# A closing bias moved into the top-k tiles, and the first attention with GpSimd's half sums ahead of its product and the output bias as a TensorE product

## The chip, the cores and the metric

The kernel runs on one core of a Trainium2 chip, in one launch. The time is device microseconds. A core has five engines that run their own queues in order and meet only at semaphores: TensorE (PE; its weight loads are shown as PEld), VectorE (DVE), ScalarE (ACT), GpSimd (POOL) and SyncE (SP, which here only issues transfers).

## The reference

The input x has 2 sequences of 1024 rows of 256 numbers; the context has 2 x 77 rows of 192. Four layers are added to x one after the other, each on a layer norm of x:

```python
x = x + _L0_xattn_ref(_layernorm(x), ctx, Wq, bq, Wkv, bkv, Wo, bo)     # 16 heads of 16, softmax over 77 keys
x = x + _L0_ffn_ref(_layernorm(x), Wg, W1, b1, Wo, bo)                  # top 2 of 8 experts, gated, 512 wide
x = x + _L1_xattn_ref(_layernorm(x), ctx, masks, ...)                   # 4 heads, top 32 of 77 keys, FiLM, s4d, FFN
x = x + _L1_ffn_ref(_layernorm(x), w_gate, w_expert, b_expert)          # top 1 of 8 with capacity 100
```

The first attention ends with `attention @ Wo + bo`: this `bo` (L0_xattn_bo) is the output bias that the change moves. The third layer takes for every row and head the 32 largest of 77 scores, turns the attention into a scale and a shift (FiLM) around a long convolution (s4d, done by Fourier transforms), runs a feed-forward part of 1024 hidden units, and ends with `layernorm(xt) * g_norm_out + b_norm_out`: this `b_norm_out` is the closing bias. The experts' first bias `b1` (8 rows of 1024) is a second operand that matters here, since the change puts `bo` beside it.

## The kernel before, in words

X lies in the core's memory for the whole kernel as 16 tiles of 128 rows. The work is in stages A to F; between some of them all engines meet at a barrier (`stage_end`). Every engine's program is written out by hand, in order; nothing is scheduled by a planner. So an instruction stands where its line puts it, and a wait holds up all that is behind it on its engine.

**Stage A, the first attention.** The loop runs over 32 units u (or steps S): 4 blocks j of 4 tiles, each with 2 groups of 8 heads, so 8 units to a block. For a unit:
- TensorE makes the scores (`scores_A`).
- VectorE takes the maximum (L1642) and the difference (L1646).
- ScalarE makes the exponential (L1075).
- GpSimd halves the row for the sum: it copies the middle column (L1360) and adds the two halves (L1361) into `hsum`.
- VectorE sums what is left (`total`, L1634) and takes the reciprocal (L1636).
- GpSimd multiplies the probabilities by it (L1355, "the product").
- TensorE, three units later, transposes the probabilities (`turn_P`, L526).

In GpSimd's step S the product of unit S-1 stands first, then the copy and the half sum of unit S, then in 16 of the units `bias_A` (L1339), which adds the output bias to one tile of X. `hsum` is one buffer. After units 5 and 9 GpSimd also makes the rstd for the next blocks' layer norm (L1317 to L1322); ScalarE waits for it before it normalises (L1037). VectorE's program for unit u is: maximum and difference of u, `total(u - 1)`, layer-norm statistics in some units, `split_bias` in units 17, 21 and 25, and `add_A`, which adds the projected attention in PSUM to X (L1599) in two units of each block from the second on. `add_A` waits for `xbA`, the count of tiles that have their bias. TensorE does, beside scores and transposes, the queries of the next block, the transposes of the normalised rows z (L492 and, for the next stage, L563), `values` and `project` (products with Wo). Nearly all products share line L470, a helper.

`split_bias` cuts the experts' bias rows (`b1s`, three copies of 8 rows at partitions 0, 32 and 64) into three bf16 parts in `b1r` (L1607, L1609, and the remainder by L1531), so that stage B can add them with a bf16 product: weights `picked` (a one at the rows of the tile's expert), moving operand `b1r`. SyncE loads the biases near the start of its queue, behind X and ahead of the experts' weights, and waits for `b1r_ready` before it loads the parameters that take the place of `b1s`.

**Stage C, the top-k tiles.** For each of 16 tiles VectorE searches the 32 largest of 77 in four rounds (MAX8 L2023, MATCH_REPLACE8 L2033). GpSimd per tile: weights (L1461, waiting for ScalarE's exponentials; L1464, waiting for VectorE's L2045; L1466; L1470, for which TensorE waits to transpose at L820), then FiLM on the tile before (L1477, L1479), in two steps the sum and difference of folded tiles (L1486, 1024 elements), and the normalised rows xn (L1492). X is not written in this stage; the last reader of its tiles here is the layer norm that writes U.

**Stage D and E.** After a barrier VectorE multiplies spectra (many instructions of 128x1024 at L1531), TensorE makes Fourier products, and GpSimd adds the closing bias (`rows[:, BNO]`) to the 16 tiles of X (L1507), counted by `xbE`. The tiles are needed later, in `norm_E`.

## Time and profile before

| what | value |
|---|---|
| median of 3 runs | 807.37 us (803.51 to 812.75) |
| profiled execution, its own time | 804.53 us |
| its span | 802.7 us |
| mean granted TensorE clock | 0.92 of full |
| busy, share of the span | PE 83%, PEld 47%, DVE 69%, ACT 39%, POOL 50% |
| chain that ended last | PE 42%, DVE 32%, POOL 9%, ACT 7%, issue 5%, DMA 3% |

The span is that of the profiled execution from its first to its last instruction; the execution's own time is 1.8 us more. Busy is the time in which an engine had an instruction in work; TensorE's ends are modelled, since its products overlap. The chain is followed back from the last instruction, at each step to what released it, so it says which engine was waited for. The granted clock is TensorE's, as a share of 2.4 GHz. A unit of stage A below is named by VectorE's difference (L1646): unit 0 is at 24.4 us, unit 31 at 132.25 us.

### The profile page before, as it was taken

The page shows a single profiled execution, that of the slowest core. Times are in us where ns is not written, and L with a number is a line of the kernel's source. Part 1 is how long each engine was busy: PE and PEld are TensorE (multiplying, and loading weights), DVE is VectorE, ACT ScalarE, POOL GpSimd, SP SyncE. Part 2 cuts the span into 40 slices and gives each one's busy share as a digit, 9 for nine tenths or more (in the row PEclk, how much of TensorE's full clock was granted, in tenths as well). Part 3 has the DMA queues.
Part 4 walks back from the last instruction along what each step waited for, and adds up shares of the span by engine and source line. Part 5 has one row for each costly group of instructions (what it writes and reads, how often), then busy time and mean ns, then how long its engine had stood idle before and what let it go on. Part 6 is the DMA issues. An engine that isn't in the chain of part 4 may idle for free.

```text
span 802.7 us, 10821 instructions
## 1 busy us (share of the span) xinstructions
PE 668.8 (83%) x3380; PEld 376.3 (47%) x3380; DVE 553.8 (69%) x1694; ACT 311.6 (39%) x686; POOL 402.4 (50%) x466
## 2 busy tenths in 40 slices
PE   4879878718899898999898699875967999899971
PEld 3435435514445454545486344324423655557651
DVE  4778886393993947572587999994964994825266
ACT  2566545302828373732122577781202220031110
POOL 3789857024988787872203467975900211202120
PEclk9999999657999999999899799897996999999986
DMA  8940001111222122224790000201000000000003
GB/s 219 374 125 1 1 23 48 52 53 66 67 79 93 63 83 74 83 87 122 284 358 1 1 2 6 100 2 52 1 0 0 2 0 1 0 1 0 1 0 105
DMA packets 33087, 52.77 MB, mean 66 GB/s; under 512 B 8718, under 2 KB 21582, under 8 KB 32776
## 3 DMA queue, kind: packets, MB, share of 16 engines
q1 hardware_dynamic: 28040, 36.75, 13.8%
q0 software_dynamic: 4992, 15.34, 5.6%
q8 instruction: 28, 0.46, 0.2%
q14 instruction: 27, 0.22, 0.1%
HBM read 36.61 MB, written 15.47 MB: 65 GB/s over the span
## 4 chain that ended last, share of the span: by engine, by line
PE 42%; DVE 32%; POOL 9%; ACT 7%; issue 5%; DMA 3%; POOLq 1%; SPq 0%; DVEq 0%; ACTq 0%
PE ps L470 38%; DVE arena L1531 6%; DVE arena L2033 5%; DVE arena L2023 3%; DVE kp L1531 3%; POOL arena L1355 3%; POOL arena L1361 2%; ACT L1148 1%; DVE arena L1634 1%; DVE arena L1883 1%; ACT arena L991 1%; PE ps L776 1%; DVE X L1537 1%; ACT L1162 1%; DMA arena<-scr_g 1%
## 5 line engine op out<-in xcount | busy, mean ns | idle before, releaser
L470 PE MATMUL ps<-arena 64*32 64x32 f32 (+10 forms) x2344 | 483.7, 395 | 29.6 <-DVE arena L1820 8.7
L470 PEld LDWEIGHTS ps<-arena 64*32 64x32 f32 (+7 forms) x2344 | 227.4, 152 | 217.3 <-issue 157.7
L991 ACT ACTIVATE arena<-ps 128x512 f32<-128x512 f32 (+4 forms) x252 | 120.7, 492 | 247.4 <-PE ps L470 115.2
L331 POOL TENSOR_SCALAR rstd<-mv 128x1 f32<-128x1 f32 (+2 forms) x30 | 13.8, 458 | 225.7 <-DVE mv L325 161.8
L1883 DVE TENSOR_TENSOR arena<-ps,arena 128x512 f32<-128x512 f32 x39 | 26.9, 690 | 74.2 <-ACT arena L1148 72.4
L1404 POOL DMA_INDIRECT scr_g<-arena,destU x39 | 49.5, 1270 | 34.9 <-DVE arena L1883 25.7
L1395 POOL DMA_INDIRECT arena<-scr_z,idsU x39 | 49.1, 1260 | 22.6 <-PE ps L706 10.7
L1148 ACT ACTIVATE arena<-ps 128x512 f32<-128x512 f32 x39 | 23.3, 598 | 82.8 <-PE ps L470 82.6
L2033 DVE MATCH_REPLACE8 arena<-arena 128x77 f32<-128x77 f32 x256 | 54.1, 222 | 0.0
L1288 ACT ACTIVATE arena<-ps,b1p 128x512 f32<-128x512 f32 x32 | 22.0, 687 | 74.6 <-PE ps L470 74.6
L1355 POOL TENSOR_TENSOR arena<-arena 128x616 f32<-128x616 f32 x32 | 40.3, 1258 | 20.8 <-DVE arena L1636 19.3
L2023 DVE MAX8 arena<-arena 128x8 f32<-128x77 f32 x256 | 41.7, 224 | 1.9 <-ACT arena L1194 1.9
L1531 DVE TENSOR_TENSOR arena<-arena 128x1024 f32<-128x1024 f32 (+10 forms) x47 | 42.1, 895 | 0.8
L1531 DVE TENSOR_TENSOR arena<-arena,kp 128x1024 f32<-128x1024 f32 (+1 forms) x36 | 40.8, 1151 | 0.6
L470 PE MATMUL ps<-b1r,picked 72*128 72x512 bf16 x78 | 30.1, 386 | 8.8 <-DVE arena L1883 4.9
L1075 ACT ACTIVATE arena<-arena 128x616 f32<-128x616 f32 x32 | 22.9, 716 | 33.5 <-DVE arena L1646 33.5
L526 PE MATMUL ps<-ident,arena 128*128 128x128 f32 (+1 forms) x160 | 25.5, 292 | 10.0 <-POOL arena L1355 5.4
L470 PE MATMUL ps<-wof,arena 128*128 128x256 f32 x128 | 31.8, 395 | 0.0
L1642 DVE TENSOR_REDUCE arena<-ps 128x8 f32<-128x616 f32 x32 | 24.8, 776 | 7.5 <-PE ps L470 7.5
L333 POOL TENSOR_TENSOR rstd<-rstd,neghalf 128x1 f32<-128x1 f32 (+2 forms) x30 | 28.2, 940 | 2.5
L1507 POOL TENSOR_TENSOR X<-X,rows 128x256 f32<-128x256 f32 x16 | 25.6, 1638 | 6.6 <-POOLq L316 6.6
L336 DVE TENSOR_SCALAR arena<-X,mv,rstd 128x256 f32<-128x256 f32 x48 | 21.0, 497 | 11.1 <-POOL rstd L333 11.1
(207 smaller groups left out, 1008.9 us busy)
## 6 DMA issues: line engine op xcount, KB each, us to landing
arena<-in_w1t SPq DMA_DIRECT2D x8, 1024.0 KB, 14.0
arena<-scr_g SPq DMA_DIRECT2D x8, 1024.0 KB, 8.2
X<-in_x SPq DMA_DIRECT2D x2, 1024.0 KB, 6.3
scr_z<-arena SPq DMA_DIRECT2D x4, 512.0 KB, 2.9
arena<-in_c_dftf SPq DMA_DIRECT2D x1, 2048.0 KB, 15.6
arena<-in_L_xattn_W SPq DMA_DIRECT2D x2, 1024.0 KB, 6.3
out<-X SPq DMA_DIRECT2D x16, 128.0 KB, 1.8
scr_k<-arena SPq DMA_DIRECT2D x4, 256.0 KB, 4.6
```

Source lines behind the costliest of these rows:

```text
L333: p.tensor_tensor(rstd[:, at:at + n], rstd[:, at:at + n], neghalf[:, 0:n], ALU.pow).then_inc(s[signal], 1)
L470: return pe.matmul(o, l, r, start=first, stop=final)
L991: return a.activation(o, i, ACT.Copy)
L1148: a.activation(sig[:, u % 2, :], bank(2 * (u % 2) + 1), ACT.Sigmoid).then_inc(s["sig_ready"], 1)
L1355: p.tensor_tensor(pv, pv, smA[:, u % PBUF, :].unsqueeze(2).broadcast_to([P, HG, S2]), ALU.mult)\
L1395: p.indirect_dma_start(xg[:, st % 2, :], None, scr_z, bass.IndirectOffsetOnAxis(ap=idsU[:, st:st + 1], axis=0))\
L1404: p.indirect_dma_start(scr_g, bass.IndirectOffsetOnAxis(ap=destU[:, u:u + 1], axis=0), gt[:, u % 2, :], None).then_inc(s[f"gs{u % 2}"], 16)
L1507: p.tensor_tensor(X[:, n, :], X[:, n, :], rows[:, BNO, :], ALU.add).then_inc(s["xbE"], 1)
L1531: own.done(v.tensor_tensor(o, x, y, op))
L1883: v.tensor_tensor(gt[:, u % 2, :], bank(2 * (u % 2)), sig[:, u % 2, :], ALU.mult).then_inc(s["g_ready"], 1)
L2023: own.done(v.max(top[:, par, h, 8 * r:8 * r + 8], hv(cur)[:, h, :]))
L2033: ins = v.match_replace(hv(Rr)[:, h, :], top[:, par, h, 8 * r:8 * r + 8], hv(cur)[:, h, :], TAKEN)
```

## The change

Four things are edited together.

1. The output bias of the first attention. `bias_A` and its 16 adds go. Instead `b1r` gets one row more in front of each copy of the experts' rows (73 rows, not 72), and L0_xattn_bo is loaded there, three times, with 256 of the row's columns. `project` starts each tile's PSUM group with a bf16 product of `borow` (a one at rows 0, 32 and 64) and `b1r[:, 0:D]`. The bias row is no longer in `rows`. `project` now waits for `b1r_ready`, and `split_bias` is called in units 5, 7 and 10.
2. GpSimd's order in a step: copy and half sum of unit S first, then the product of S-1.
3. `hsum` has two buffers, the second in a part of `kp`. Before the copy GpSimd waits for `probs_sum` of unit S-2. `rstd_A` and `rstd_B` stay behind the product of units 5, 9, 16 and 24.
4. The closing bias: the 16 adds stand in the top-k tiles, each behind the xn of its tile.

```diff
@@ sync
             for i in range(3):
-                load(sp, b1s[0][32 * i:32 * i + NE, :], d["b1e"], "b1_in")
-            for i, name in enumerate(("L0_xattn_bo", "L0_ffn_bo", "L1_xattn_g_norm_in", "L1_xattn_b_norm_in",
+                load(sp, b1s[0][32 * i + 1:32 * i + 1 + NE, :], d["b1e"], "b1_in")
+                load(sp, b1s[0][32 * i:32 * i + 1, 0:D], d["L0_xattn_bo"].rearrange("(o d) -> o d", o=1), "b1_in")
+            for i, name in enumerate(("L0_ffn_bo", "L1_xattn_g_norm_in", "L1_xattn_b_norm_in",
@@ tensor, project
+                pe.wait_ge(s["b1r_ready"], 3)
                 pe.wait_ge(s["oT_sb"], 2 * j + 2)
                 for t in (2 * pair, 2 * pair + 1):
+                    o = ps[:, 6 + pair, (t % 2) * D:(t % 2) * D + D]
+                    mm(o, borow[:].broadcast_to([BROWS, P]), b1r[:, 0:D], True, False)
                     for g in range(2):
-                        ins = mm(ps[:, 6 + pair, (t % 2) * D:(t % 2) * D + D], OT[:, g, t * P:(t + 1) * P], wo0[:, g, :],
-                                 g == 0, g == 1)
+                        ins = mm(o, OT[:, g, t * P:(t + 1) * P], wo0[:, g, :], False, g == 1)
@@ gpsimd, start
+            own.done(p.memset(borow[:], 0.0))
+            own.settle()
+            for i in range(3):
+                own.done(p.memset(borow[32 * i:32 * i + 1, :], 1.0))
@@ gpsimd, stage A
             for S in range(NU + 1):
-                if S:
-                    u = S - 1
-                    p.wait_ge(s["probs_sum"], u + 1)
-                    ...
                 if S < NU:
                     p.wait_ge(s["probs_exp"], S + 1)
-                    ...
+                    if S >= 2:
+                        p.wait_ge(s["probs_sum"], S - 1)
+                    pv, hs = Pb[:, S % PBUF, :].rearrange("p (h k) -> p h k", h=HG), hsum[S % 2]
+                    p.tensor_copy(hs[:, :, H2:H2 + 1], pv[:, :, H2:H2 + 1]).then_inc(s["half_ready"], 1)
+                    p.tensor_tensor(hs[:, :, 0:H2], pv[:, :, 0:H2], pv[:, :, H2 + 1:S2], ALU.add).then_inc(s["half_ready"], 1)
                 if S == 0:
                     continue
-                if u == 0:
-                    p.wait_ge(s["rows_in"], 16 * 9)
-                if u < 5:
-                    bias_A(u)
-                ...
+                u = S - 1
+                p.wait_ge(s["probs_sum"], u + 1)
+                pv = Pb[:, u % PBUF, :].rearrange("p (h k) -> p h k", h=HG)
+                p.tensor_tensor(pv, pv, smA[:, u % PBUF, :].unsqueeze(2).broadcast_to([P, HG, S2]), ALU.mult)\
+                    .then_inc(s["probs_norm"], 1)
+                if u in (5, 9):
+                    rstd_A(2 + u // 9)
@@ gpsimd, top-k tiles
                         p.tensor_tensor(xn[:, n % 2, :], U[:, n, :], rstd[:, TB + n:TB + n + 1].broadcast_to([P, D]), ALU.mult)\
                             .then_inc(s["xn_ready"], 1)
+                        p.tensor_tensor(X[:, n, :], X[:, n, :], rows[:, BNO, :], ALU.add).then_inc(s["xbE"], 1)
@@ gpsimd, stage E
-                for n in range(NT):
-                    p.tensor_tensor(X[:, n, :], X[:, n, :], rows[:, BNO, :], ALU.add).then_inc(s["xbE"], 1)
@@ vector
-                v.wait_ge(s["xbA"], n + 2)
                 v.tensor_tensor(X[:, n:n + 2, :], X[:, n:n + 2, :], bank(6 + pair).rearrange("p (t n) -> p t n", t=2), ALU.add)\
...
-                own.done(v.tensor_reduce(smA[:, u % PBUF, :], hsum, AX, ALU.add))
+                own.done(v.tensor_reduce(smA[:, u % PBUF, :], hsum[u % 2], AX, ALU.add))
...
-                if u in (17, 21, 25):
-                    split_bias(u // 4 - 4)
+                if u in (5, 7, 10):
+                    split_bias((5, 7, 10).index(u))
```

## Rows read from the trace of the kernel before

**Rows 1.** Windows of stage A, blocks 0 to 3: length; busy PE, PEld, DVE, ACT, POOL; clock; DMA.
```profile
24.40:48.65 24.25, 20.17 (x109) 10.34 (x107) 18.23 (x39) 12.46 (x21) 19.39 (x30) 0.93 1.01 371
48.65:76.46 27.81, 24.91 (x144) 13.61 (x145) 20.79 (x44) 20.30 (x36) 24.93 (x38) 1.00 0.01 2
76.46:109.80 33.34, 25.52 (x143) 13.38 (x142) 26.96 (x47) 16.61 (x30) 24.69 (x34) 0.95 0.00 0
109.80:132.25 22.45, 20.02 (x127) 12.18 (x129) 17.93 (x37) 14.17 (x25) 16.24 (x24) 1.00 0.19 62
```

**Rows 2.** Timeline of GpSimd in a unit with the bias add: start us, us, instruction.
```profile
66.28 1.22 POOL L1355 TENSOR_TENSOR arena<-arena 128x616 f32<-128x616 f32 x1
...
68.37 0.74 POOL L1339 TENSOR_TENSOR X<-X,rows 128x256 f32<-128x256 f32 x1
69.25 1.22 POOL L1355 TENSOR_TENSOR arena<-arena 128x616 f32<-128x616 f32 x1
```

**Rows 3.** Timeline of a unit behind the last bias add; in brackets idle time, releaser.
```profile
123.56 0.72 ACT L1075 ACTIVATE arena<-arena 128x616 f32<-128x616 f32 x1 [1.46 <-DVE arena L1646]
...
124.29 0.48 DVE L1634 TENSOR_REDUCE arena<-arena 128x8 f32<-128x312 f32 x1 [0.76 <-POOL arena L1361]
...
125.08 1.22 POOL L1355 TENSOR_TENSOR arena<-arena 128x616 f32<-128x616 f32 x1 [0.83 <-DVE arena L1636]
```

**Rows 4.** Timeline of TensorE in block 1.
```profile
67.50 0.79 PE L470 MATMUL ps<-arena 64*128 64x308 f32 x4
68.22 0.77 PE L526 MATMUL ps<-ident,arena 128*128 128x128 f32 x5
68.83 1.89 PE L470 MATMUL ps<-wo,arena 128*128 128x256 f32 x8
...
72.07 2.65 PE L470 MATMUL ps<-arena 128*32 128x512 f32 x20
...
75.25 1.88 PE L470 MATMUL ps<-arena,wq 128*128 128x512 f32 x4
```

**Rows 5.** Instructions on the tile b1r: count, duration in ns min/median/max.
```profile
L1609 DVE CAST b1r<-kp x3: 637/684/1592, 81.2 to 114.5; 8x1024 bf16<-8x1024 f32 x2, 72x1024 bf16<-72x1024 f32 x1
L1531 DVE TENSOR_TENSOR kp<-kp,b1r x2: 1893/2006/2118, 81.8 to 98.7; 72x1024 f32<-72x1024 f32 x1, 8x1024 f32<-8x1024 f32 x1
L1607 DVE CAST b1r<-kp x1: 683/683/683, 96.3 to 96.3; 32x1024 bf16<-32x1024 f32 x1
```

**Rows 6.** Waits around units 7 and 21, and the window behind the second.
```profile
48.74 1.09 ACT L1037 ACTIVATE arena<-X,arena,rstd 128x256 f32<-128x256 f32 x2 [4.88 <-POOL arena L1322]
...
104.00:108.00 4.00, 3.94 (x20) 1.29 (x20) 2.82 (x7) 0.78 (x2) 3.17 (x6) 0.57 0.00 0
...
104.06 1.09 PE L563 MATMUL ps<-ident,arena 128*128 128x128 f32 x4 [4.53 <-DVE X L1599]
105.08 3.84 PE L470 MATMUL ps<-arena 128*32 128x512 f32 x20
```

**Rows 7.** Timeline of TensorE: a bf16 bias product of 512 columns, and the next.
```profile
213.19 0.38 PE L470 MATMUL ps<-b1r,picked 72*128 72x512 bf16 x1
213.41 1.88 PE L470 MATMUL ps<-arena 128*128 x4
```

**Rows 8.** Timelines of the top-k stage: a wait of GpSimd, one of TensorE.
```profile
498.73 0.84 POOL L1461 TENSOR_TENSOR arena<-arena 128x308 f32<-128x308 f32 x1 [0.80 <-ACT arena L1228]
...
509.08 0.50 PE L820 MATMUL ps<-ident,arena 128*77 128x128 f32 x1 [0.73 <-POOL arena L1470]
```

**Rows 9.** Stage D: GpSimd's adds, VectorE's products beside and behind them, TensorE.
```profile
555.33 25.65 POOL L1507 TENSOR_TENSOR X<-X,rows 128x256 f32<-128x256 f32 x16 [6.58 <-POOLq L316]
...
L1531 DVE TENSOR_TENSOR arena<-arena,kp 128x1024 f32<-128x1024 f32 x4 | 6.6, 1661 | 0.1
...
L1531 DVE TENSOR_TENSOR arena<-arena,kp 128x1024 f32<-128x1024 f32 x2 | 2.4, 1223 | 0.0
...
589.31 8.57 PE L470 MATMUL ps<-arena 128*128 128x512 f32 x16 [3.25 <-DVE arena L2124]
```

More of the change, by code:

```diff
@@ L53 @@
 SCAT = 4
-BROWS = 2 * 32 + NE
+BROWS = 2 * 32 + 1 + NE
 HUGE = 1.0e30
@@ L117, in build @@
         wx = sb("wx", [P, KD, D + NE])
-        rows = sb("rows", [P, 9, D])
-        BO0, BOF, GNI, BNI, GNO, BNO, B2, DSKIP, BEXP = range(9)
+        rows = sb("rows", [P, 8, D])
+        BOF, GNI, BNI, GNO, BNO, B2, DSKIP, BEXP = range(8)
         mgate = sb("mgate", [P, 1])
@@ L152, in build @@
         H2 = S2 // 2
-        hsum = ra.take(HG, H2 + 1)
+        hsum0 = ra.take(HG, H2 + 1)
         kvT = OT.rearrange("p g n -> p (g n)")[:, 0:4 * NB * S2].rearrange("p (a b n) -> p a b n", a=2, b=2)
@@ L207, in build @@
         erow = sb("erow", [BROWS, 1])
+        borow = sb("borow", [BROWS, 1], BF16)
         onerow = onesb[0:1, :]
@@ L219, in build @@
         kpf = kp[:].rearrange("p a b -> p (a b)")
+        hsum = (hsum0, kpf[:, 16 * P:16 * P + HG * (H2 + 1)].rearrange("p (h k) -> p h k", h=HG))
         tmpD = kpf[:, 0:2 * 4 * D].rearrange("p (i m n) -> p i m n", i=2, m=4)
@@ L423, in _ @@
                                  KT[32 * j:32 * j + 32, :, :]).then_inc(s["k_out"], 16)
-                sp.wait_ge(s["xbA"], 2 * NT)
+                sp.wait_ge(s["xbA"], NT)
                 for i in range(2):
@@ L1334, in rstd_B @@
                     ln_shift(TB + 4 * j, "lnB_stats", j + 1, "lnB_rstd")
-            def bias_A(T):
-                p.wait_ge(s["zA_ready"], T + 1)
-                p.tensor_tensor(X[:, T, :], X[:, T, :], rows[:, BO0, :], ALU.add).then_inc(s["xbA"], 1)
             rstd_A(0)
@@ L1379, in _ @@
                 rstd_B(2)
+            p.wait_ge(s["rows_in"], 16 * 8)
             stage_end("gpsimd", p)
@@ L1413, in _ @@
                         else:
-                            p.wait_ge(s["xbA"], NT + T)
+                            p.wait_ge(s["xbA"], T)
                         own.done(p.tensor_scalar(bof[:, T % 2, :], rows[:, BOF, :], cw[:, NSEL, T:T + 1], None, ALU.mult))
@@ L1602, in split_bias @@
             def split_bias(i):
-                v.wait_ge(s["b1_in"], 48)
+                v.wait_ge(s["b1_in"], 16 * 6)
                 x, rest = b1s[i % 2], b1s[(i + 1) % 2]
@@ L2357, in host_inputs @@
     o["b1e"] = A["L0_ffn_b1"]
-    o["c_erow"] = np.where(p[:BROWS] % 32 < NE, p[:BROWS] % 32, -1).astype(np.float32)[:, None]
+    o["c_erow"] = np.where(p[:BROWS] % 32 <= NE, p[:BROWS] % 32 - 1, -1).astype(np.float32)[:, None]
     o["c_iota"] = np.tile(np.arange(P, dtype=np.float32), (P, 1))
```

14 lines of the change are left out of this document (removed).

## The prediction

> **What bounds the kernel now.** The change touches three stretches: the first attention (stage A), the top-k tiles, and the head of stage D. The windows between VectorE's subtractions of units 0, 8, 16, 24 and 31 [rows 1] give blocks 0 to 2 of stage A 24.3, 27.8 and 33.3 us, and seven units of block 3 22.5. GpSimd's timeline of one unit [rows 2] shows why it looks like the limit: product 1.22 us, then column copy and half sum 1.01, bias add 0.74, and products start 2.97 us apart. Behind the last bias add the unit is as long, for another reason [rows 3]: GpSimd idles 0.83 us for VectorE's reciprocal (1.22 + 1.01 + 0.83 = 3.06), VectorE before that 0.76 us for the half sum. They wait for each other in turn. TensorE's timeline [rows 4] gives its demand: scores 0.72 us to the next start, five transposes 0.61, a projection pair 1.89, values 2.65 - 0.79 = 1.86, queries 1.88. For a block with everything in it (block 2, with 16 more transposes of z at 0.61 / 5) that is 5.8 + 4.9 + 3.8 + 3.7 + 3.8 + 2.0 = 24.0 us, 3.0 per unit. So TensorE is full at GpSimd's pace: work taken off GpSimd alone frees little in blocks 1 and 3. Block 2 is 9.3 us longer than TensorE's 24.0, and there something can be won.
>
> **Part 1, the split of the expert bias, from units 17, 21, 25 to 5, 7, 10.** Its work on VectorE [rows 5]: first part 0.64 + 2.12 = 2.8 us; second 0.68 + 1.59 + 1.89 = 4.2; third 0.68. Where it stands now TensorE idles 4.53 us for X behind the second part, comes back in a window of 4 us with a granted clock of 0.57 (mostly 1.2 GHz), and takes 3.84 us [rows 6] for the 20 instructions that took 2.65 in [rows 4]. Block 2 loses 2.8 + 4.2 + 1.2 = 8.2 us by it. Without, 25.1 us are left, just above the 24.0 that TensorE needs, so I take back all 8.2; the bounds are 4.5 (the gap alone) and 9.3.
> Block 0 has to pay. VectorE is busy 18.2 of its 24.3 us [rows 1]. Unit 5's part stands in front of the next unit's maximum, with ScalarE, GpSimd and TensorE behind it: 0 to 2.8, I take 2.8, since the neighbouring units run tight. At unit 7 ScalarE stands 4.88 us for GpSimd's rstd [rows 6], with the next exponential behind it, so the half sum comes late whatever VectorE does. The second part lies beside that wait: 0 to 4.2, I take 0.3. The third stands where TensorE is full: 0. TensorE will idle longer in block 0 than now; slow clock behind a longer gap costs between 0 and 4 x (1 - 0.57) = 1.7 us per window as in [rows 6]: 1.0. Block 0: + 4.1.
> One of the two short casts in [rows 5] takes 1.59 us where its like takes 0.68. The Trainium skill, SBUF — State Buffer, section "Who interferes with whom", has a cast of VectorE and any GpSimd instruction on one exclusive pair of ports, the later one blocked until the earlier ends; the 1.59 agrees. By that rule the first part's cast, too, can stand behind a GpSimd product of 1.22 us in its new place, and the sum below would be - 4.8 instead of - 6.0; with one cast in two seen so [rows 5], I give it half of the forecast's chance, and its 802.6 lies inside the forecast's spread.
>
> **Part 2, GpSimd's order and the second buffer.** The half sum of unit S goes ahead of the product of S-1 and needs only the exponential. In [rows 3] that ends at 124.28 us (123.56 + 0.72), while the half sum stood behind the product of 125.08. The mutual wait of 0.83 us goes, and the pace falls to that of the slowest engine: VectorE busy 17.9 us in seven units, 2.6 each; TensorE 3.0. So block 3 gains nothing. Block 1, at 27.8 against a demand of 24.0 less a z transpose, holds some stall from unit 8 on: 0 to 3.8, I take 2.0. The product comes up to 1.0 us later; TensorE transposes it three units later, which hides it, and without these units of lead it would cost 1.0 each. The wait on the sum of S-2 before the copy (for the buffer) is met already: the product of S-2, one round earlier, waited for the same count.
>
> **Part 3, the output bias.** Removed: 16 adds of 0.74 us on GpSimd, units 0 to 17, and VectorE's wait for them. TensorE being full, they are worth nothing beyond the 2.0 above. Added: 16 bf16 products of 256 columns. A bf16 product of 512 columns is followed by the next after 0.22 us [rows 7]: lower bound 0.11; upper bound a float32 step of 256 columns, 1.89 / 8 = 0.24 [rows 4]. I take 0.13, by the bf16 row as the same kind: + 2.1, all of it on TensorE's path (12 products in blocks 1 to 3, 4 in the tail). The projection's wait for b1r is met by unit 10; the first projection stands at unit 13. SyncE issues three 1 KB loads more and one of 128 KB less, in the first 13 us; the split needs them at about 40 us, and what is queued behind comes about 1 us later and is needed in later stages: 0. The four small memsets stand in GpSimd's wait for the first statistics: 0; were that cover gone, some 0.1 us each. SyncE's wait for b1r is met 50 us sooner; its parameter loads find no user before the next stage: 0.
>
> **Part 4, the closing bias.** In the top-k stage VectorE sets the pace; GpSimd idles 0.80 us before L1461 in a settled tile [rows 8], so an add of 0.74 hides. Not around 503 to 513 us, where two adds of 1024 elements fill GpSimd and TensorE idles 0.73 us for its L1470 [rows 8]: + 0.7, and + 0.5 at the last tile, which has no next tile to catch up in. Bounds: 0, and at the 25.65 / 16 = 1.60 us that each takes now [rows 9], 16 x (1.60 - 0.80) = 12.8. I take + 1.2, since GpSimd's other adds there run beside the same VectorE searches at their plain length.
> In stage D the adds cover 25.65 us, and VectorE's products of 1024 elements take 1.66 us beside them, 1.22 behind them [rows 9]; 14 of about that size make some 6 us. TensorE waits only 3.25 us for VectorE, at 589.31 [rows 9], and then sets that step itself: - 3.2 (bounds 0 and - 3.25).
>
> **Sum.** Stage A - 8.2 + 4.1 - 2.0 + 2.1 = - 4.0; top-k + 1.2; D - 3.2: - 6.0 us. The profiled execution took 804.53 us: 798.5. The median of the three runs, 807.37, is 2.8 above it: 801.4, so 801.
>
> **Rivals.** (a) Full gain: TensorE's steps in [rows 4] are stretched, and VectorE's 2.6 us per unit is the pace. Units 8 to 31 less the 2.0 counted: 23 x 0.4 = 9 us, 7 more, and the bias products hide: total about - 14, 793. For: ends of TensorE's rows are modelled. Against: its steps stand back to back, with no idle time at their side. 0.22.
> (b) Slower: the second part is not covered, and TensorE falls to 1.2 GHz before block 1, where it is the limit. Block 0 pays 7.0, two slow windows 3.4, block 1 gains nothing and block 2 only the gap of 4.5: 7.0 + 3.4 - 4.5 + 2.1 = + 8.0, with - 2.0 elsewhere + 6, 813. It decides from where block 0 and 1 lose more than the 8.2 of block 2. For: the slow return of [rows 6]. Against: ScalarE's wait is there anyway. The Trainium skill, TensorE: Matmul & The Clock Gate, section "What's actually happening", has the throttled clock as the default that activity lifts; the 0.57 behind the gap agrees. 0.10.
> (c) The new order does nothing, and the mutual wait stays in another guise: block 1's 2.0 and about 2 of block 2 are lost, 805. Against: the exponential of [rows 3] ends 0.8 us ahead of the product that it had to follow. 0.13.
> (d) The forecast: 0.55.
>
> **Numbers.** A measurement of this kernel tells about 1% (8 us) from no change. Below 799.3: (a) and a third of (d), 0.40. Above 815.4: half of (b) and the bound of part 4, 0.06. Between: 0.54. Leaving out half of (a) and most of (b): 792 to 810.
>
> **What would show it.** Right: block 2 at about 25.5 us, block 0 at 28 to 29, TensorE's gap of 4.5 us gone and one of about 5 us near unit 7; TensorE without idle in blocks 1 and 3; in D VectorE's products at 1.22 throughout and TensorE's wait of 3.25 gone; the top-k stage about 1 us longer. Wrong: units well below 3 us (a), a low granted clock in block 1 (b), or half sums that start no sooner after the exponential (c).

## The result, and the profile after

The kernel after takes **800.21 us**, the median of 11 runs (798.55 to 804.27); the kernel before took 808.37 beside it. The ratio is 0.9915, with a 95% interval of 0.9889 to 0.9941. Run a second time, unchanged, beside the experiments (a2_after), it gave 0.9939 [0.9912, 0.9965]. So it is some 0.6 to 0.9% faster, 5 to 7 us. The prediction said 801.0, with a range of 792 to 810. The profiled execution took 798.55 us against 804.53 before, 6.0 less, and the sum of the prediction's terms was -6.0. Most of what follows is about why that agreement is partly luck.

From the page of after, the busy times and the chain:

```profile
PE 667.7 (84%) x3396; PEld 376.2 (47%) x3396; DVE 545.6 (68%) x1694; ACT 312.1 (39%) x686; POOL 377.0 (47%) x454
...
PE 48%; DVE 27%; ACT 8%; POOL 7%; issue 5%; DMA 3%; POOLq 1%; SPq 0%; DVEq 0%; ACTq 0%
```

GpSimd has lost the sixteen adds of stage A and the stretched adds of stage D. Of these only 0.7 us, in stage A, had been on the chain of the kernel before. Where the 6 us came from is seen by laying the two traces' landmarks side by side. Each row gives the length of a stretch; stage A is counted between VectorE's subtractions of unit 0 and unit 31, as in [rows 1].

| stretch | before | after | difference |
|---|---|---|---|
| start to unit 0 | 24.41 | 23.61 | -0.80 |
| units 0 to 31 | 107.84 | 102.60 | -5.24 |
| unit 31 to the first gather by ids | 46.62 | 47.51 | +0.89 |
| to the first tile of top-k | 267.22 | 267.85 | +0.63 |
| top-k, to TensorE's first column of stage D | 109.16 | 110.97 | +1.81 |
| stage D, to TensorE's first product of E | 58.24 | 55.13 | -3.11 |
| the rest | 189.21 | 188.93 | -0.28 |

The windows of stage A in after answer to [rows 1]; the columns are the same (length, busy PE, PEld, DVE, ACT, POOL, clock, DMA):

```profile
23.61:49.68 26.07, 20.14 (x108) 10.02 (x106) 23.19 (x44) 12.34 (x21) 19.41 (x24) 0.87 0.99 355
49.68:79.78 30.10, 26.05 (x146) 14.44 (x147) 21.81 (x46) 19.89 (x36) 21.08 (x33) 0.94 0.04 12
79.78:104.85 25.07, 24.43 (x149) 13.58 (x148) 20.21 (x42) 17.34 (x31) 19.22 (x29) 1.00 0.06 22
104.85:126.21 21.36, 19.76 (x127) 12.30 (x125) 17.41 (x36) 13.57 (x25) 16.26 (x26) 1.00 0.08 26
```

Block 2 gained 8.3 us. The prediction had 7.7: 8.2 for the split, less 0.5 for four bias products. Blocks 0 and 1 together lost 4.1 where 2.6 was predicted. Block 0 is 1.8 longer, not 4.1; its first unit alone came out 1.1 us shorter (2.63 against 3.69), and there traces of one program differ by as much. Block 1, forecast 1.5 shorter, is 2.3 longer. Block 3, forecast 0.5 longer by its bias products, is 1.1 shorter.

GpSimd's new order is visible at once. This is the timeline of after in block 3, answering to [rows 3]: start us, us, instruction, and in brackets the idle time with what ended it.

```profile
117.29 0.71 ACT L1080 ACTIVATE arena<-arena 128x616 f32<-128x616 f32 x1
...
118.06 0.20 POOL L1360 COPY arena<-arena 128x8 f32<-128x8 f32 x1
118.21 0.83 POOL L1361 TENSOR_TENSOR arena<-arena 128x304 f32<-128x304 f32 x1
119.01 1.21 POOL L1367 TENSOR_TENSOR arena<-arena 128x616 f32<-128x616 f32 x1
...
119.27 0.47 DVE L1628 TENSOR_REDUCE arena<-arena 128x8 f32<-128x312 f32 x1
```

The exponential ends at 118.00, the half sum starts right behind it, and the product follows without the wait of 0.83 us for the reciprocal. The mutual wait is gone, so rival (c) is out for this place.

**Where blocks 0 and 1 lose.** The same timeline of after, units 5 to 9:

```profile
39.10 0.64 DVE L1603 CAST b1r<-kp 73x1024 bf16<-73x1024 f32 x1
39.77 1.89 DVE L1526 TENSOR_TENSOR kp<-kp,b1r 73x1024 f32<-73x1024 f32 x1
...
40.53 2.20 POOL L1367 TENSOR_TENSOR arena<-arena 128x616 f32<-128x616 f32 x1
...
42.79 1.33 PE L529 MATMUL ps<-ident,arena 128*128 128x128 f32 x5 [2.90 <-POOL arena L1367]
44.05 4.54 PE L473 MATMUL ps<-arena 128*32 128x512 f32 x20
...
46.10 0.74 DVE L1601 CAST b1r<-kp 32x1024 bf16<-32x1024 f32 x1
46.26 0.67 POOL L1326 TENSOR_SCALAR rstd<-mv 128x4 f32<-128x4 f32 x1
47.01 0.64 POOL L1327 TENSOR_SCALAR arena<-mv 128x4 f32<-128x4 f32 x1
47.59 1.22 DVE L1526 TENSOR_TENSOR kp<-kp,b1r 9x1024 f32<-9x1024 f32 x1
47.73 1.98 POOL L1329 TENSOR_TENSOR rstd<-rstd,neghalf 128x4 f32<-128x4 f32 x1
...
50.02 1.09 ACT L1042 ACTIVATE arena<-X,arena,rstd 128x256 f32<-128x256 f32 x2 [5.94 <-POOL arena L1331]
51.73 1.30 PE L529 MATMUL ps<-ident,arena 128*128 128x128 f32 x5 [3.14 <-ACT arena L996]
52.83 2.90 PE L473 MATMUL ps<-arena,wq 128*128 128x512 f32 x4
```

Read it in order. The first part of the split (39.10) makes TensorE late by one gap of 2.90 us (it is 1.66 at this place in e2 below, which has no split here), since GpSimd's product beside the subtraction takes 2.20 us instead of 1.22. TensorE comes back slow: the 20 value products take 4.54 us instead of 2.65 [rows 4]. The second part (46.10) lies beside GpSimd's rstd chain, as predicted. But it is not free there, because the chain itself stretches: 0.67, 0.64 and 1.98 us, where the same instructions before took 0.24, 0.23 and 1.04. ScalarE waits 5.94 us for it instead of 4.88 [rows 6]. TensorE idles 3.14 us and is slow again: its four query products take 2.90 us, against 1.88 in [rows 4]. In the trace of before TensorE came to the same place from a gap nearly as long and was not slow; the granted clock from 50 to 54 us was 1.00:

```profile
50.45 0.74 PE L526 MATMUL ps<-ident,arena 128*128 128x128 f32 x5 [2.69 <-ACT arena L991]
51.03 1.88 PE L470 MATMUL ps<-arena,wq 128*128 128x512 f32 x4
```

### The profile page after: what moved, and what is told of

The parts are those of the page before. It is cut to its first block, busy times and chain, and to the rows that moved or that the text cites. A ratio compares the mean times of both kernels' runs of the same rounds, so it can differ in the third digit from the quotient of the medians.

```text
span 796.6 us, 10872 instructions
## 1 busy us (share of the span) xinstructions
PE 667.7 (84%) x3396; PEld 376.2 (47%) x3396; DVE 545.6 (68%) x1694; ACT 312.1 (39%) x686; POOL 377.0 (47%) x454
## 4 chain that ended last, share of the span: by engine, by line
PE 48%; DVE 27%; ACT 8%; POOL 7%; issue 5%; DMA 3%; POOLq 1%; SPq 0%; DVEq 0%; ACTq 0%
PE ps L473 43%; DVE arena L2027 5%; DVE arena L1526 4%; DVE arena L2017 3%; DVE kp L1526 2%; ACT L1153 1%; PE ps L529 1%; POOL arena L1367 1%; DVE arena L1877 1%; ACT arena L996 1%; DVE arena L338 1%; DVE X L1532 1%; DMA arena<-scr_g 1%; ACT L1167 1%; DVE arena L1640 1%
## 5 line engine op out<-in xcount | busy, mean ns | idle before, releaser
L996 ACT ACTIVATE arena<-ps 128x512 f32<-128x512 f32 (+4 forms) x252 | 121.1, 492 | 255.0 <-PE ps L473 111.3
L1526 DVE TENSOR_TENSOR arena<-arena 128x1024 f32<-128x1024 f32 (+10 forms) x47 | 40.1, 854 | 0.9
L1526 DVE TENSOR_TENSOR arena<-arena,kp 128x1024 f32<-128x1024 f32 (+1 forms) x36 | 39.0, 1101 | 0.6
L473 PE MATMUL ps<-b1r,picked 73*128 73x512 bf16 x78 | 30.1, 386 | 8.9 <-DVE arena L1877 4.7
L529 PEld LDWEIGHTS ps<-ident,arena 128*128 128x128 f32 (+1 forms) x160 | 17.4, 144 | 25.2 <-issue 13.8
```

The source lines that it names most:

```text
L473: return pe.matmul(o, l, r, start=first, stop=final)
L529: ins = pe.transpose(o, Pb[:, u % PBUF, c * P:c * P + m], ident[:])
L996: return a.activation(o, i, ACT.Copy)
L1526: own.done(v.tensor_tensor(o, x, y, op))
```

## The experiments

Twelve runs were made, eleven of other kernels and one of after again, each with five rounds beside the kernel before. Stage A (units 0 to 31) is read from each trace, block by block, in us; the clock column is the granted clock of block 0. "u7+u8" is the time from the subtraction of unit 7 to that of unit 9, where the rstd chain stands. Ratios are to the kernel before.

| kernel | block 0 | 1 | 2 | 3 | sum | clock | u7+u8 | median, ratio [95%] |
|---|---|---|---|---|---|---|---|---|
| before | 24.24 | 27.81 | 33.34 | 22.45 | 107.84 | 0.93 | 9.25 | |
| e3_closing (same stage A) | 24.64 | 29.00 | 34.48 | 22.38 | 110.50 | 0.93 | 10.59 | 805.89, 0.9998 [0.9969, 1.0027] |
| e1_split_early | 28.70 | 27.38 | 26.21 | 21.93 | 104.22 | 0.88 | 11.81 | 800.94, 0.9957 [0.9936, 0.9979] |
| e2_order | 22.19 | 29.49 | 29.53 | 21.31 | 102.52 | 1.00 | 11.67 | 798.71, 0.9931 [0.9909, 0.9952] |
| e12_order_closing | 25.31 | 26.36 | 28.69 | 21.30 | 101.66 | 0.93 | 10.01 | 798.26, 0.9898 [0.9872, 0.9924] |
| e4_old_order | 30.40 | 27.19 | 25.50 | 21.91 | 105.00 | 0.88 | 11.63 | 801.99, 0.9948 [0.9923, 0.9974] |
| after | 26.07 | 30.10 | 25.07 | 21.36 | 102.60 | 0.87 | 12.68 | 800.21, 0.9915 [0.9889, 0.9941] |
| a2_after | 25.20 | 30.95 | 25.07 | 21.37 | 102.59 | 0.93 | 13.52 | 801.82, 0.9939 [0.9912, 0.9965] |
| e5_no_bias_products | 26.07 | 29.78 | 24.63 | 20.91 | 101.39 | 0.87 | 12.81 | 801.28, 0.9922 [0.9888, 0.9955] |
| e8_no_second_part | 26.80 | 27.12 | 25.07 | 21.37 | 100.36 | 0.87 | 9.36 | 797.57, 0.9878 [0.9844, 0.9912] |
| e6_small_split | 26.82 | 25.50 | 25.08 | 21.36 | 98.76 | 0.87 | 9.36 | 797.19, 0.9867 [0.9829, 0.9905] |
| e9_bo_at_start | 25.05 | 26.18 | 25.07 | 21.36 | 97.66 | 0.93 | 9.35 | 796.36, 0.9862 [0.9819, 0.9905] |
| e10_adds_apart | 23.82 | 25.98 | 25.07 | 21.42 | 96.29 | 0.93 | 9.35 | 794.96, 0.9831 [0.9783, 0.9878] |
| e11_adds_in_E | 22.99 | 25.96 | 25.07 | 21.37 | 95.39 | 0.93 | 9.36 | 801.34, 0.9927 [0.9894, 0.9959] |

Before and e3 run the same stage A and differ by 2.7 us, most of it in blocks 1 and 2, where e3's granted clock is lower (0.94 and 0.90, against 1.00 and 0.95). e9, e10 and e11 share theirs too and differ by 2.3, nearly all in block 0. So a single trace's stage A is good to some 2.5 us. Blocks 2 and 3 of one program repeat to 0.1 once the split is out of block 2; e2 and e12, which keep it there, differ by 0.8, as VectorE's cast took 1.35 us in one and 0.69 in the other.

**e1_split_early.** The move of the split alone.

```diff
-                if u in (17, 21, 25):
-                    split_bias(u // 4 - 4)
+                if u in (5, 7, 10):
+                    split_bias((5, 7, 10).index(u))
```

> The kernel before with one thing changed: the three parts of the split of the expert bias stand at units 5, 7 and 10 instead of 17, 21 and 25. My theory (T1): the stages' gain of the change in stage A is this move alone, 8.2 us out of block 2, against a loss in blocks 0 and 1 that is larger than the 4.1 us predicted, since the second part is not covered by GpSimd's rstd at unit 7: it slows that chain and TensorE comes back on the slow clock twice. Block 2 should fall from 33.3 to 25 to 26 us, blocks 0 and 1 together should grow by 4 to 7, and the whole should be 2 to 4 us faster than before. Rival (T2): the order of GpSimd and the freed adds carry the gain, and the split only moves its cost: 0 to 2 us slower than before.

Measured: 0.9957, about 3.5 us faster. Its windows of blocks 0 and 2:

```profile
23.93:52.63 28.70, 20.68 (x114) 10.85 (x113) 24.57 (x43) 15.42 (x28) 23.41 (x33) 0.88 0.86 317
...
80.01:106.22 26.21, 23.83 (x143) 12.92 (x142) 20.19 (x42) 16.96 (x30) 21.96 (x34) 1.00 0.06 21
```

Block 2 falls by 7.1 us, block 0 pays 4.5, block 1 gives 0.4. It is not always GpSimd that stretches. Here its power keeps its 1.04 us (only the small multiply behind it takes 0.54 instead of 0.20), and VectorE's subtraction in the second part takes 2.27:

```profile
47.87 1.04 POOL L1320 TENSOR_TENSOR rstd<-rstd,neghalf 128x4 f32<-128x4 f32 x1
...
49.48 1.21 POOL L1355 TENSOR_TENSOR arena<-arena 128x616 f32<-128x616 f32 x1
49.50 2.27 DVE L1531 TENSOR_TENSOR kp<-kp,b1r 8x1024 f32<-8x1024 f32 x1
```

The first theory holds for the move taken alone: TensorE's late return in block 2 was VectorE's, and the split in block 0 costs more than half of it back. Which of the two engines stretches goes by which began first: GpSimd's product began 0.02 us ahead of the subtraction, and the subtraction ended 1.08 us behind the product's end. In after the power began 0.14 us behind VectorE's subtraction (47.73 against 47.59), and ended 0.90 behind its end.

**e2_order.** GpSimd's order and the two buffers alone; the bias adds, the split and the closing adds stay.

```diff
+                    if S >= 2:
+                        p.wait_ge(s["probs_sum"], S - 1)
+                    pv, hs = ..., hsum[S % 2]
...
+                u = S - 1
+                p.wait_ge(s["probs_sum"], u + 1)
...
+                    .then_inc(s["probs_norm"], 1)
```

> The kernel before with GpSimd's half sum ahead of its product and two buffers for the half sums; the bias adds, the split and the closing adds stay where they were. T1: TensorE is the pace of blocks 1 and 3, so the order gives 0 to 2 us, of which most in blocks 0 and 1 and about 1 in block 3; with the bias adds still there GpSimd's unit of 2.97 us stays. Rival T2: the mutual wait of 0.83 us per unit was the bound, and units 18 to 31 fall by up to 0.8 us each: 8 us or more faster.

Measured: 0.9931, 5.6 us faster, where 0 to 2 was expected. My theory fell here, and with it the prediction's price of the order. The rival's 0.8 us in each of units 18 to 31 does not come either: block 3 falls by 1.1 in all, and block 1, from unit 9 on, by 0.3. The window of block 2 in e2:

```profile
75.35:104.88 29.53, 24.30 (x145) 13.32 (x144) 26.67 (x47) 17.19 (x31) 23.79 (x33) 1.00 0.00 1
```

Block 2 falls from 33.34 to 29.53 with the split still in it, and block 3 by 1.1. Why block 2? In the kernel before, VectorE comes to the split late. These are its three half-sum waits ahead of the split of unit 21, in the timeline of before:

```profile
89.63 0.48 DVE L1634 TENSOR_REDUCE arena<-arena 128x8 f32<-128x312 f32 x1 [1.90 <-POOL arena L1361]
...
92.60 0.48 DVE L1634 TENSOR_REDUCE arena<-arena 128x8 f32<-128x312 f32 x1 [0.76 <-POOL arena L1361]
...
95.58 0.48 DVE L1634 TENSOR_REDUCE arena<-arena 128x8 f32<-128x312 f32 x1 [0.76 <-POOL arena L1361]
```

and the same place in e2, with TensorE's wait for X behind it:

```profile
87.15 0.48 DVE L1636 TENSOR_REDUCE arena<-arena 128x8 f32<-128x312 f32 x1 [0.95 <-POOL arena L1358]
...
89.94 0.48 DVE L1636 TENSOR_REDUCE arena<-kp 128x8 f32<-128x312 f32 x1 [0.57 <-POOL kp L1358]
...
92.07 0.47 DVE L1636 TENSOR_REDUCE arena<-arena 128x8 f32<-128x312 f32 x1
...
100.77 0.66 PE L564 MATMUL ps<-ident,arena 128*128 128x128 f32 x4 [2.15 <-DVE X L1601]
101.36 2.65 PE L471 MATMUL ps<-arena 128*32 128x512 f32 x20
```

In these three units VectorE waits 1.52 us instead of 3.42, it is earlier against TensorE, and the gap is 2.15 us instead of the 4.53 of [rows 6]. Behind the shorter gap the clock was full (the window 98 to 106 us shows 1.00) and the 20 products took 2.65 us instead of 3.84. So of the 8.2 us that the prediction booked on the split, 2.4 of the gap and 1.2 of the clock go in this trace with the mutual wait ahead of it, though the split stays. A second trace of the same stage A, e12, gets there another way:

```profile
93.38 1.33 PE L527 MATMUL ps<-ident,arena 128*128 128x128 f32 x5 [1.31 <-POOL arena L1364]
...
102.22 0.60 PE L564 MATMUL ps<-ident,arena 128*128 128x128 f32 x4
```

Here TensorE came back slow from a gap of 1.31 us some 9 us earlier (e2 had 1.30 there and the full clock). Later by that, and with VectorE's cast 0.66 us shorter, it no longer waited for X. Block 2 took 28.69 us against 29.53, so it falls either way.

Block 0 is 2.0 us shorter in e2. Of this 1.1 is its first unit, where traces of one program differ (2.63 us here, 4.24 in e12). Units 2 and 6 give another 1.6: they took 2.23 and 2.12 us instead of 2.97, in e12 as well. Units 3 and 7 take 0.8 back, and unit 8, in block 1, 2.0 (7.87 us against 5.87).

**e4_old_order.** The kernel after with the product ahead of the half sum again.

```diff
+                if S:
+                    u = S - 1
+                    p.wait_ge(s["probs_sum"], u + 1)
...
                 if S < NU:
                     p.wait_ge(s["probs_exp"], S + 1)
-                    if S >= 2:
-                        p.wait_ge(s["probs_sum"], S - 1)
```

> The kernel after with GpSimd's old order, the product of the last unit ahead of the half sum of this one; the two buffers stay. T1: TensorE sets the pace with the bias adds gone, and the order is worth 0 to 2 us: between 800 and 802. Rival T2: the order carries the gain of blocks 1 and 3: the mutual wait returns in all 32 units, and the time goes back to 806 or more.

Measured: 0.9948, in stage A 2.4 us more than after, within the 0 to 2 expected by the medians (801.99 against 800.21 and 801.82). Block 2 changes by 0.4 and block 3 by 0.5. With the split gone from block 2 the order has little left to shorten there. The order is worth 5.6 us alone. Beside the moved split it is worth 0.2 to 1.8 by the medians and 1.0 in blocks 2 and 3, which repeat best: the two edits remove the same wait. In this trace GpSimd's chain at the second part kept its 0.23, 0.23 and 1.04 us, as in e1, and units 7 and 8 still took 11.63 us, with a gap of 4.55 on TensorE.

**e3_closing.** Only the closing bias is moved.

```diff
                             .then_inc(s["xn_ready"], 1)
+                        p.tensor_tensor(X[:, n, :], X[:, n, :], rows[:, BNO, :], ALU.add).then_inc(s["xbE"], 1)
...
-                for n in range(NT):
-                    p.tensor_tensor(X[:, n, :], X[:, n, :], rows[:, BNO, :], ALU.add).then_inc(s["xbE"], 1)
```

> The kernel before with only the closing bias moved into the top-k tiles. T1: stage D gives 3.1 us, the top-k stage costs 1.7: 1.4 us faster, between 0.5 and 2.5. Rival T2: VectorE's stretched products in stage D, some 6 us, come back as a whole: 4 us faster. Rival T3: the adds push the top-k tiles by more than that once they run at another phase of stage D's loads: no gain, or slower.

Measured: 0.9998 with an interval of 0.6%; it cannot tell 1.4 us from nothing. The stages say more. From the first tile of top-k to TensorE's first column of stage D, the nine traces with the move that were read so take 110.74 to 111.84 us (mean 111.3), the four without (before, e1, e2, e11) 108.36 to 109.67 (mean 109.2): the adds cost 2.1. Stage D takes 55.12 to 55.15 us in the nine, and 58.24, 56.75, 60.21 and 60.23 in the four: 3.7 less in the mean. That leaves a gain of about 1.6 us, with a wide spread: the two stretches together take 165.11 to 169.88 us in the four and 165.88 to 166.98 in the nine. e12 against e2, which differ by this edit alone, has 0.9898 against 0.9931, 2.7 us for the move, with overlapping intervals. So stage D's wait and its end are shown, the gain of the move as a whole is not settled.

**a2_after.** The kernel after, unchanged.

> The kernel after, unchanged, as the companion of the runs beside it and as a second trace of the same program. Both theories expect what was measured first, 0.9915 of the kernel before, within its interval.

Measured: 0.9939, within the first interval. Its stage A is 102.59 us, though by other blocks: 25.20 and 30.95 in place of 26.07 and 30.10. In unit 8 (8.49 us here, 7.64 there) the four query products took 3.62 us here and 2.90 there, by the slow clock.

**e5_no_bias_products.** After without the 16 bf16 products; the output bias is left out.

```diff
-                    mm(o, borow[:].broadcast_to([BROWS, P]), b1r[:, 0:D], True, False)
                     for g in range(2):
-                        ins = mm(o, OT[:, g, t * P:(t + 1) * P], wo0[:, g, :], False, g == 1)
+                        ins = mm(o, OT[:, g, t * P:(t + 1) * P], wo0[:, g, :], g == 0, g == 1)
```

> The kernel after without the 16 bf16 products that add the output bias (it is left out altogether; the split stays). The trace of after has them at 0.11 us each. T1 (TensorE is the pace of blocks 1 to 3, the last four products stand in the tail): 1.3 to 2 us faster than after. Rival T2 (TensorE has room): 0 to 0.5 us.

Measured: blocks 1, 2 and 3 are 0.32, 0.44 and 0.45 us shorter, four products each, so 0.11 us per product, and nothing hides them. With the four of the tail that is 1.65 us, an estimate at the same 0.11. The medians (801.28 against 801.82) are too close to tell it. So TensorE is the pace where these products stand, as the first theory has it.

**e8_no_second_part.** After with the second part of the split, at unit 7, left out; the third part then starts from the whole row, so the sum of the parts is wrong.

```diff
                 if i == 1:
-                    own.done(v.tensor_copy(b1r[32:64, :], x[32:64, :]))
+                    return
...
-                v.tensor_copy(b1r[part, :], x[part, :]).then_inc(s["b1r_ready"], 1)
+                v.tensor_copy(b1r[part, :], x[part, :]).then_inc(s["b1r_ready"], 1 + i // 2)
```

> The kernel after with the second part of the split left out (the cast, the copy and the subtraction at unit 7; the residual term is wrong by it). The prediction had this part covered: 0.3 us. T1: it costs 2 to 4 us there, 1.5 to 1.9 of it by slowing GpSimd's rstd chain and the rest by a longer slow clock. Rival T2: as predicted, 0 to 0.5 us, and the long gap of 7.64 us between units 8 and 9 stays.

Measured: 0.9878; 4.3 us under a2_after in the medians, 2.2 in the sum of stage A, and 3.3 to 4.2 in u7+u8 (9.36 against 12.68 and 13.52). The timeline of e8 at the same place:

```profile
48.54 0.23 POOL L1326 TENSOR_SCALAR rstd<-mv 128x4 f32<-128x4 f32 x1
48.85 0.23 POOL L1327 TENSOR_SCALAR arena<-mv 128x4 f32<-128x4 f32 x1
49.16 1.04 POOL L1329 TENSOR_TENSOR rstd<-rstd,neghalf 128x4 f32<-128x4 f32 x1
...
50.52 1.09 ACT L1042 ACTIVATE arena<-X,arena,rstd 128x256 f32<-128x256 f32 x2 [4.16 <-POOL arena L1331]
...
52.23 0.74 PE L529 MATMUL ps<-ident,arena 128*128 128x128 f32 x5 [1.54 <-ACT arena L996]
52.81 1.88 PE L473 MATMUL ps<-arena,wq 128*128 128x512 f32 x4
```

The chain is back at 0.23, 0.23 and 1.04 us, ScalarE waits 4.16, TensorE 1.54 instead of 3.14, and its queries take 1.88 us instead of 2.90. The second part lies beside the wait and lengthens it by 1.8 us of chain. The rest is the clock, and that part is less certain than one pair of traces makes it look. With the second part at unit 7 (after, a2, e1, e4, e5) the four query products took 2.90 to 3.62 us each time; without it they took 1.88 in seven traces of nine, but 2.71 in e3 and 3.40 in e2. Units 7 and 8 took 11.63 to 13.52 us with it and 9.24 to 11.67 without. The comparison leaves one thing mixed: taking the part out removes both its load on VectorE and its effect on GpSimd. But VectorE had nothing to do for its maximum in e8 until 50.81 (it idled 2.46 us for TensorE), so its load alone, 2.65 us, would nearly have fitted.

**e6_small_split.** The output bias is split by itself, 65 rows of 256 columns, at unit 3; the expert bias, split in the same three parts, stands where VectorE idles at the end of stage A.

```diff
+            def split_bo():
+                ...
+                own.done(v.tensor_copy(bor[:], a))
+                tt(b, a, bor[:], ALU.subtract)
+                own.done(v.tensor_copy(bor[32:64, :], b[32:64, :]))
+                own.done(v.tensor_copy(bor[64:65, :], b[64:65, :]))
+                tt(a[64:65, :], b[64:65, :], bor[64:65, :], ALU.subtract)
+                v.tensor_copy(bor[64:65, :], a[64:65, :]).then_inc(s["b1r_ready"], 1)
...
-                if u in (5, 7, 10):
-                    split_bias((5, 7, 10).index(u))
+                if u == 3:
+                    split_bo()
...
+            for i in range(3):
+                split_bias(i)
             add_A(NBLK - 1, 0)
```

> The kernel after with the output bias split by itself, 65 rows of 256 columns, at unit 3, and the split of the expert bias in VectorE's idle 8.4 us at the end of the first attention. T1: blocks 0 and 1 lose the 4.5 us that the split of the whole tile cost there against the kernel with the new order alone, block 2 stays at 25: 3 to 5 us faster than after. Rival T2: the two long gaps of block 0 and 1 are GpSimd's rstd chain and the slow clock, which come whatever VectorE does: 0 to 1 us. Rival T3: the late split delays the parameter loads of the next stage, and what is won is given back there.

Measured: 0.9867, 4.6 us under a2_after in the medians and 3.8 in stage A. The next stage's first gather comes 3 to 5 us sooner as well (168.89 against 171.98 and 173.72), so the late split gives nothing back. Unit 3 now takes 6.52 us instead of 4.00.

**e9_bo_at_start.** e6 with the small split ahead of VectorE's first statistics; the bias comes by one load that ScalarE issues.

```diff
+            load(a, bos[:, 0, :], d["L0_xattn_bo"].rearrange("(o d) -> o d", o=1).broadcast_to([65, D]), "b1_in")
...
+            split_bo()
             stats_A(0, range(4))
...
-                if u == 3:
-                    split_bo()
```

> The small split of the output bias of e6, but done before VectorE's first statistics, where VectorE stands 8.4 us for X; the bias comes by one load that ScalarE issues at the start. T1: e6 still paid about 2.5 us for the small split at unit 3 (its unit took 6.52 us against 4.00 us in after and in e2), so the span from unit 0 to unit 31 falls from 98.8 to 96 to 98 us, and the whole is 5 to 7 us faster than after (a ratio to the kernel before near 0.985). Rival T2: the long wait for GpSimd's rstd at units 7 to 9 takes up whatever unit 3 gives, as the kernel with the new order alone showed it (7.87 us at unit 8): the same as e6. Rival T3: the load and the split ahead of the statistics delay X, and the first subtraction comes later by 1 us or more.

Measured: 0.9862, the same as e6 within the interval. Stage A fell by 1.1 us in the trace, and in e10 and e11, which share it, by 2.5 and 3.4. But unit 0 came at 26.20, 25.30 and 25.13 us instead of 23.82, which takes most of it away. All three expectations were partly met; whether the later start is the split's or chance isn't settled (e12, without any of it, started at 25.92, e8 at 24.84).

**e10_adds_apart.** e9, with the closing adds of tiles 8, 9, 10 and 15 back at the head of stage E's work.

```diff
-                        p.tensor_tensor(X[:, n, :], X[:, n, :], rows[:, BNO, :], ALU.add).then_inc(s["xbE"], 1)
+                        if n not in (8, 9, 10, 15):
+                            p.tensor_tensor(X[:, n, :], X[:, n, :], rows[:, BNO, :], ALU.add).then_inc(s["xbE"], 1)
...
+                for n in (8, 9, 10, 15):
+                    p.tensor_tensor(X[:, n, :], X[:, n, :], rows[:, BNO, :], ALU.add).then_inc(s["xbE"], 1)
...
-                    v.wait_ge(s["xbE"], n + 1)
+                    v.wait_ge(s["xbE"], NT)
```

> e9 with the closing adds of the four tiles 8, 9, 10 and 15, where GpSimd is full or which end the top-k stage, put back at the head of the last-but-one stage's GpSimd work; twelve stay in the top-k tiles. T1: the top-k stage gets back 1 to 2 us of the 2.1 that the sixteen adds cost, and the next stage keeps its 55 us: 1 to 2 us faster than e9. Rival T2: the top-k stage's loss is spread over all tiles, and the next stage loses again: no gain.

Measured: 794.96 us, 0.9831 [0.9783, 0.9878], the fastest of all kernels here, 1.2% to 2.2% under the kernel before. Against e9 the top-k stage got back 0.7 us (110.18 against 110.91) and stage D stayed at 55.14. The tiles show more than that 0.7: between TensorE's transposes of neighbouring tiles (L827) the steps that took 7.69, 7.56 and 5.35 us in e9 take 6.99, 6.88 and 4.96 here, 1.8 less. The last ten products of the stage then took 6.03 us instead of 4.55, behind a gap of 1.92, with a granted clock of 0.76 from 535 to 542 us. The step before the last tile stayed at 5.38 (4.87 where no add stands in this stage), so the add of tile 15 was not the one that costs there. The step from e9 to e10 is inside the intervals; the step from after is not.

**e11_adds_in_E.** e9 with all sixteen adds back in stage E.

```diff
-                        p.tensor_tensor(X[:, n, :], X[:, n, :], rows[:, BNO, :], ALU.add).then_inc(s["xbE"], 1)
...
+                for n in range(NT):
+                    p.tensor_tensor(X[:, n, :], X[:, n, :], rows[:, BNO, :], ALU.add).then_inc(s["xbE"], 1)
```

> e9 with all sixteen closing adds back where they were before the change, at the head of GpSimd's work of the next stage. T1: the move is worth about 1.2 us (top-k 2.1 us shorter, the next stage 3.3 us longer): 0.5 to 2 us slower than e9. Rival T2: the move as a whole is worth nothing, as its run alone measured (0.9998): the same as e9.

Measured: 801.34 us, 0.9927, so 5.0 us slower than e9 in the medians where 0.5 to 2 was expected. Its traced execution (794.77 us) is the fastest of its twelve, and in the trace stage D is 5.1 longer and top-k 1.5 shorter than in e9, 3.6 together. By the intervals the move is worth something beside the small split, while e3 alone showed nothing; how much stays open. In stage D of e11 TensorE's wait for VectorE is back:

```profile
550.77 24.62 PE L475 MATMUL ps<-arena 128*128 128x512 f32 x52
578.00 8.83 PE L475 MATMUL ps<-arena 128*128 128x512 f32 x16 [2.60 <-DVE arena L2137]
```

**e12_order_closing.** The change without its moved split and without the bias products: the order, the two buffers, the closing adds. The edit is that of e2 and e3 together.

> The kernel before with GpSimd's new order and its two buffers, and the closing bias in the top-k tiles: the change without its moved split and without the output bias on TensorE. T1: with the new order in place the moved split only shifts 4.5 us from block 2 into blocks 0 and 1, so this kernel is level with after: 0.990 to 0.995 of before, 102.5 us from unit 0 to unit 31. Rival T2: the parts are additive, each worth what its own run gave, and the moved split is worth 3 us or more here too: 3 us or more slower than after, near 0.997.

Measured: 798.26 us, 0.9898 [0.9872, 0.9924]; level with after or a little better. Its block 2:

```profile
77.59:106.28 28.69, 25.59 (x145) 14.72 (x144) 25.76 (x48) 17.31 (x31) 24.56 (x33) 0.94 0.00 1
```

Block 2 still holds the split, 3.6 us over after's 25.07. Blocks 0 and 1 hold 51.7 us against after's 56.2. With the order in place, the moved split and the bias on TensorE, taken together, return nothing that these runs can tell.

## Why the prediction was right, point by point

**The sum** was right: -6.0 predicted, -6.0 between the profiled executions, and the ratio is inside the 1% that was called no change. The full gain of rival (a) would have needed units well below 3 us; blocks 2 and 3 stand at 3.1. The terms were not all right: the second part of the split and its slow clock cost more than forecast, and the order gave more in block 3. Agreement to 0.1 us is luck besides, since stage A of one program differs by some 2.5 us between traces. One sum of the prediction is off: rival (a)'s terms (-6.0, 7 more, and the 2.1 hidden) add up to -15, not -14.

**Block 2, -8.2.** Measured -8.3. The size holds, the cause only in part: e2 takes 3.8 us of it with the split left in place, e1 7.1 with the order left in place, and together they give 8.3, not 10.9. The forecast booked all of it on the split, and only rival (c) gave the order about 2 of it.

**Block 0's first part, +2.8.** Measured 2.65 (unit 5: 4.77 us instead of 2.12). Right. By the Trainium skill, SBUF — State Buffer, section "Who interferes with whom", I had given half of the forecast's chance to a cast that waits behind a GpSimd product. The cast took 0.64 us, so here it did not wait; what stretched was GpSimd's product, to 2.20 us.

**The second part, +0.3, "beside that wait".** This is the step that failed. It cost 3.3 to 4.2 us in u7+u8 by e8, 2.2 in the whole of stage A; 1.8 of it is the chain, shown, and the rest the clock, which fell there in two traces without the part as well. The cover was there in time. But the work under it and the work that made the cover hindered each other, and in after the cover itself grew. That is not the only way to pay: in e1 and e4 the chain grew by 0.34 us only, VectorE's subtraction took 2.27 us, and units 7 and 8 were still 11.81 and 11.63 us long. The prediction took the length of a wait as given that another engine was making at that very moment.

**Slow clock, +1.0.** It fell twice: 4.54 us instead of 2.65, where the kernel before had 3.55 at the same place, and 2.90 instead of 1.88. That is 1.0 each on these products, 2.0 in all, the second of it behind the failed step. Rival (b) described this, and blocks 0 and 1 did lose 4.1 us; but block 2 gained in full, so its end did not come.

**The order, -2.0 in block 1 and 0 in block 3.** Mis-sized, and misplaced. From unit 9 on, block 1 goes from 21.9 us (27.81 less the 5.87 of unit 8) to 21.7 in e12: 0.3. Block 3 goes from 22.4 to 21.3: 1.1. Block 2 gives 3.8. The argument that TensorE is full at GpSimd's pace is borne out by block 1 and by e5. What it missed is a block where TensorE waits for VectorE, and VectorE had waited for GpSimd. In block 3 TensorE was not full either. Before, it waited once for GpSimd's product:

```profile
123.38 0.77 PE L526 MATMUL ps<-ident,arena 128*128 128x128 f32 x5 [1.45 <-POOL arena L1355]
```

In after it waits 0.45 and 0.61 us there.

**The bias products, +2.1.** Measured 0.11 us each, 1.2 in blocks 1 to 3 and an estimated 1.65 with the tail. Right in kind, 0.4 too high. That they lie open on TensorE's path is shown.

**Top-k, +1.2.** Measured +1.8 in this pair, 2.1 in the mean. The places were right: from one tile's transpose (L820 before, L825 after) to the next, two steps near 503 to 513 us grew from 7.02 and 6.89 us to 7.68 and 7.56, and the last from 4.87 to 5.37. In after GpSimd is busy without a break where two large adds meet, and TensorE waits (timelines of GpSimd and TensorE):

```profile
502.01 0.73 POOL L1490 TENSOR_TENSOR X<-X,rows 128x256 f32<-128x256 f32 x1
...
509.57 0.73 POOL L1490 TENSOR_TENSOR X<-X,rows 128x256 f32<-128x256 f32 x1
...
505.30 0.50 PE L825 MATMUL ps<-ident,arena 128*77 128x128 f32 x1 [0.96 <-POOL arena L1466]
512.86 0.33 PE L825 MATMUL ps<-ident,arena 128*77 128x128 f32 x1 [1.22 <-POOL arena L1466]
```

where [rows 8] had one wait of 0.73. The prediction counted one add's length at this place; there are two.

**Stage D, -3.2.** TensorE's wait is gone, and its 68 products stand in one piece:

```profile
559.38 31.45 PE L473 MATMUL ps<-arena 128*128 128x512 f32 x68
```

Before, 52 of them stood ahead of the wait, and 16 behind it [rows 9]:

```profile
562.10 23.96 PE L470 MATMUL ps<-arena 128*128 128x512 f32 x52
```

Together that took 35.78 us, so this gave 4.3, more than the wait: the 16 products behind the gap had taken 8.57 us, against an estimated 7.4 at the pace of the 68. Then 1.2 went back, since four later products took 3.31 us instead of 2.07. Net -3.1.

**Not foreseen:** the start was 0.8 us sooner, and the stretches between stage A and top-k took 1.5 more, of which an estimated 0.4 are the last four bias products; e12 shows a start 1.5 us later than before with neither the moved split nor the bias products, so the start, at least, is within what one execution differs from the next.

## What to carry to other kernels

When two edits shorten the same wait, price each with the other in place; a wait of one engine for a second can begin as the second's wait for a third, and then an edit upstream takes part of what was booked downstream. A stretch that another engine spends computing is not free cover: ask whether the work to be hidden slows the very instructions that make the stretch, above all short chains that everything waits for. Put setup work where an engine idles behind a transfer or at the end of a stage, and split off the small part that is needed early, as e6 and e9 did. When a term is smaller than what two traces of one program differ by, read it from single waits and instructions, or from several traces.

## What the runs showed of the hardware

- Small GpSimd instructions can take two to three times as long beside VectorE's casts and subtractions of 1024 columns: a 128x4 scale took 0.67 us instead of 0.23, a 128x4 power 1.98 instead of 1.04, with VectorE's operands only 9 or 32 rows high. In after each began behind VectorE's instruction and ended behind it: the first scale at 46.93 us, the cast at 46.84.
- It goes both ways, and in these cases the engine that began second paid (see e1). VectorE's subtraction of 73 rows took 1.89 us beside GpSimd, and one of 72 rows with GpSimd idle at the end of stage A in e6 took 1.22:

```profile
131.00 1.22 DVE L1529 TENSOR_TENSOR kp<-kp,b1r 72x1024 f32<-72x1024 f32 x1
```

- TensorE came back slow from gaps of 2.90 and 3.14 us in after (granted clock 0.50, the level of 1.2 GHz, from 44 to 48 us, and 0.64 from 52 to 56), and at the full clock from a gap of 2.15 us in e2. The Trainium skill, TensorE: Matmul & The Clock Gate, section "What's actually happening", has the low clock as the default that activity lifts. The trace agrees. The slow return cost 1.9 and 1.0 us here, by the durations above against [rows 4]. The length of the gap alone did not decide it: the clock was full behind 2.69 us in before, and slow behind 1.31 in e12, where e2, the same program, had 1.30 and the full clock.
